# One normalisation in place of two in a row ahead of the token routes

## The reference, cut to what matters

```python
def _layernorm(x, axis=-1, eps=1e-05):
    m = jnp.mean(x, axis=axis, keepdims=True)
    v = jnp.var(x, axis=axis, keepdims=True)
    return (x - m) / jnp.sqrt(v + eps)

def _L1_ffn_ref(x, gamma, beta, Wr, br, W1, b1, W2, b2):
    mu = jnp.mean(x, axis=-1, keepdims=True)
    var = jnp.mean(jnp.square(x - mu), axis=-1, keepdims=True)
    xn = (x - mu) * jax.lax.rsqrt(var + EPS) * gamma + beta
    logits = jnp.einsum('bsd,de->bse', xn, Wr) + br
    top_vals, top_idx = jax.lax.top_k(logits, K)          # K = 2 of E = 8
    ...                                                   # the chosen experts on xn, weighted and summed

x = x + _L0_gnn_ref(_layernorm(x, axis=-1), ...)
x = x + _L0_ffn_ref(_layernorm(x, axis=-1)[None], ...)[0]
x = x + _L1_gnn_ref(_layernorm(x, axis=-1), ...)
x = x + _L1_ffn_ref(_layernorm(x, axis=-1)[None], ...)[0]
```

## Time and profile before

| | before |
|---|---|
| median of three executions | 6341.12 us |
| the profiled execution's own time | 6339.42 us |
| its span, first to last instruction | 6337.8 us |
| TensorE busy / VectorE busy | 4515.4 us / 3970.4 us |
| ScalarE busy / GpSimd busy | 2035.9 us / 2842.5 us |
| mean granted clock of TensorE (1 is 2.4 GHz) | 0.875 |

### The profile page before, as it was taken

How to read it: one execution, slowest core, us unless ns; L and a number is a source line. 1 busy time by engine, 2 the same in 40 slices (tenths; PEclk the granted TensorE clock), 3 DMA queues, 4 the chain that set the end, 5 groups by cost and what they waited for, 6 DMA issues and landing times. The chain is left out here.

```text
span 6337.8 us, 104789 instructions
## 1 busy us (share of the span) xinstructions
PE 4515.4 (71%) x23232; PEld 3431.3 (54%) x23437; DVE 3970.4 (63%) x7274; ACT 2035.9 (32%) x4728; POOL 2842.5 (45%) x2898
## 2 busy tenths in 40 slices
PE   0688888888778888888859779355555553439990
PEld 0556666666565666666649779343344342416660
DVE  4677777777667777777766656795444445713332
ACT  0134454545324555555533323320000000314440
POOL 0066666666107777777400010007777774061116
PEclk9999999999989999999979889687767776559995
DMA  6466556556236666666420030013333332122113
GB/s 88 141 185 181 173 171 176 173 174 174 81 129 200 187 182 183 180 184 183 127 91 0 0 103 0 10 36 103 104 103 103 104 104 68 42 96 71 61 55 121
DMA packets 352764, 736.54 MB, mean 116 GB/s; under 512 B 75533, under 2 KB 193809, under 8 KB 352477
## 3 DMA queue, kind: packets, MB, share of 16 engines
q0 software_dynamic: 189824, 588.23, 31.8%
q1 hardware_dynamic: 162782, 146.70, 8.1%
HBM read 634.25 MB, written 100.43 MB: 116 GB/s over the span
## 5 line engine op out<-in xcount | busy, mean ns | idle before, releaser
L967 POOL DMA_INDIRECT rows_a<-kv_scratch,att_idx x848 | 872.6, 1029 | 971.2 <-issue 540.9
L728 POOL DMA_INDIRECT rows_a<-k_scratch,sage_sum_idx x832 | 798.0, 959 | 856.2 <-issue 852.0
L967 POOL DMA_INDIRECT rows_c<-kv_scratch,att_idx x816 | 871.5, 1068 | 353.0 <-issue 245.0
L1425 PE MATMUL ps<-rows_a 128*128 128x258 f32 x1664 | 610.9, 532 | 469.9 <-DMA rows_a<-k_scratch,sage_sum_idx 310.9
L1105 PE MATMUL ps<-attention_rows_b,att_work 128*128 x3328 | 870.4, 403 | 77.5 <-DVE att_work L1213 37.4
L1024 ACT ACTIVATE attention_rows_b<-ps x1664 | 649.2, 390 | 598.0 <-PE ps L1119 374.0
L1425 PEld LDWEIGHTS ps<-rows_a 128*128 128x128 f32 x1664 | 419.4, 264 | 661.0 <-DVE sage_rows_b L1403 410.4
L1105 PEld LDWEIGHTS ps<-attention_rows_b,att_work 128*128 128x128 f32 x3328 | 612.3, 196 | 212.3 <-issue 125.2
L1403 DVE TENSOR_TENSOR sage_rows_b<-sage_rows_b,ps 128x258 f32 x832 | 353.0, 424 | 564.3 <-PE ps L1425 370.0
L1119 PE MATMUL ps<-rows_a,att_work 128*128 128x264 f32 x1696 | 516.6, 431 | 82.0 <-DVE rows_a L1227 63.8
L1119 PE MATMUL ps<-rows_c,att_work 128*128 128x264 f32 x1632 | 504.9, 431 | 55.3 <-issue 27.4
(11 more groups left out here) (396 smaller groups left out, 9295.8 us busy)
## 6 DMA issues: line engine op xcount, KB each, us to landing
kv_scratch<-rows_c SPq DMA_DIRECT2D x100, 256.0 KB
rows_a<-kv_scratch,att_idx POOLq DMA_INDIRECT x848, 3.7
slot_in<-rows_c SPq DMA_DIRECT2D x1, 13568.0 KB
rows_a<-slot_in SPq DMA_DIRECT2D x106, 128.0 KB
slot_out<-rows_a POOLq DMA_DIRECT2D x106, 128.0 KB
rows_a<-k_scratch,sage_sum_idx POOLq DMA_INDIRECT x832, 2.7
rows_c<-kv_scratch,att_idx POOLq DMA_INDIRECT x816
h_scratch<-rows_a SPq DMA_DIRECT2D x2, 6400.0 KB
```

Source lines behind the costliest of these rows:

```text
L728: pool.indirect_dma_start(ring[:, slot, 0:D], None, table, bass.IndirectOffsetOnAxis(ap=idx[:, slot:slot + 1], axis=0)).then_inc(landed[sl ...
L967: pool.indirect_dma_start(r.halves[h][:, u, 0:KV], None, c.kv_dram[:, :], bass.IndirectOffsetOnAxis(ap=idx[:, slot:slot + 1], axis=0)).the ...
L1425: mm = pe.matmul(c.ps[:, to:to + nw], s_buf[:, q, u, :], rhs, start=True, stop=True)
```

## The change

The call of `ln_x3` goes, and `ln_tok` reads `rows_c` in its place. With `normed_twice` two small operations more make v + eps*v + eps*eps out of v. In all eight calls eps is now added on VectorE by the second operand pair of an instruction that was there (L436), and the root on ScalarE has no bias column.

```diff
@@ -399,7 +399,8 @@
-def layer_norm(c, src, dst, name, have_stats=False, gamma=None, beta=None, add_to=None):
+def layer_norm(c, src, dst, name, have_stats=False, gamma=None, beta=None, add_to=None,
+               normed_twice=False):
@@ -433,7 +434,12 @@
                 do(v.scalar_tensor_tensor(c.rstd[:, :], tmp, D / 4.0, c.rstd[:, :], ALU.mult, ALU.add))
-                do(v.tensor_scalar(c.rstd[:, :], c.rstd[:, :], 1.0 / D, None, ALU.mult))
+                if normed_twice:
+                    do(v.tensor_scalar(c.rstd[:, :], c.rstd[:, :], 1.0 / D, None, ALU.mult))
+                    do(v.tensor_scalar(tmp, c.rstd[:, :], LN_EPS, LN_EPS * LN_EPS, ALU.mult, ALU.add))
+                    do(v.tensor_tensor(c.rstd[:, :], c.rstd[:, :], tmp, ALU.add))
+                else:
+                    do(v.tensor_scalar(c.rstd[:, :], c.rstd[:, :], 1.0 / D, LN_EPS, ALU.mult, ALU.add))
                 v.sem_inc(var_ready, 1)
@@ -461,7 +467,7 @@
-                a.activation(c.rstd[:, :], c.rstd[:, :], ACT.Sqrt, bias=c.eps_col[:, 0:1]).then_inc(rooted, 1)
+                a.activation(c.rstd[:, :], c.rstd[:, :], ACT.Sqrt).then_inc(rooted, 1)
@@ -2564,8 +2570,7 @@
-            layer_norm(c, c.rows_c, c.rows_a, "ln_x3")
-            layer_norm(c, c.rows_a, c.rows_a, "ln_tok", False, L1_ffn_gamma, L1_ffn_beta)
+            layer_norm(c, c.rows_c, c.rows_a, "ln_tok", False, L1_ffn_gamma, L1_ffn_beta, normed_twice=True)
```

## The result

The changed kernel took 6315.13 us (median of 6 runs, 6313.01 to 6319.74), the kernel before 6344.64 us (6 runs, 6338.59 to 6346.97). The ratio is 0.9956, with an interval from 0.9943 to 0.9969: 28 us less, between 20 and 36. The forecast was 30.4 us less and 6310 us, with a range of 6300 to 6320 us. The time lies inside, 5 us above the value. Of these 5 us, 3.5 belong to the kernel before: with three more executions its median rose from the 6341.12 us that the forecast started from to 6344.64 us. The saving by the ratio is 2.5 us smaller than the sum, which the interval of 16 us cannot tell from nothing; what follows goes by the lengths of stages.

What follows compares the result with a forecast made beforehand. VectorE was taken to bound both normalisations, with nothing beside to hide them. -30.88 + 0.48 = -30.4 us from the profiled 6339.4 gives 6309.0; the median, 1.7 us higher, gives 6310.7, predicted as 6310 us, range 6300 to 6320.

Steps and rivals of the forecast that it cites:

- No cover: In `ln_x3` and `ln_tok` VectorE bounds both calls, busy 28.43 of 30.9 us in `ln_x3`; nothing beside could hide them.
- 30.88 us from start to start: Removing `ln_x3` saves the distance from its statistics' start to those of `ln_tok`, 5394.30 - 5363.42 us, no part hidden.
- +0.48 us added: In `ln_tok`, two small chained operations on 128x50 cost 0.23 and 0.25 us, all on the path.
- The statistics from `rows_c`: In `ln_tok`, reading `rows_c` for `rows_a` may give 0.21 us; counted 0 to -0.2, taken as 0.
- The root: ScalarE's root without bias column, eight times: between 0 and 2.7 us less in all, taken as 0.
- The clock in `expert_rows`: TensorE's clock rise at the stage's start may come earlier or later against the work: -4.5 to +4.5 us.
- rival A: A faster TensorE clock in `token_routes`: 18 us more gain, about -48 us, 6291 us; chance 3%.
- rival D: `expert_rows` stays longer at 1.2 GHz, eating the gain from 61 us of low clock: 6345 us and above; chance 1%.
- Rival C: Half the removed time comes back through a late transfer or engine: about -15 us, 6325 us; chance 3%.
- "Otherwise the same" for the stages behind the change: `token_routes`, `dispatch`, `expert_rows` and `combine` start 30.4 us earlier and are otherwise the same, save for TensorE's clock.
- Rival B: Moved VectorE and ScalarE loops reload code, 2.7 us a pass in `token_routes` and `expert_rows`: 6357 us; 4% in two outcomes.
- All windows ahead of 5363 should be the same.: A sign to check: every timeline window before the removed normalisation, at 5363 us, keeps its length.

Runs made afterwards that it cites:

- The pads: Changed kernel plus semaphore increments: TensorE 4 (6310.98 us) or 24 (6317.09 us), GpSimd 8 (6312.66 us), SyncE 4 (6311.71 us).

## Why the prediction was right, and where it was not

- **No cover.** Right. 28.43 of 30.9 us of VectorE with TensorE and GpSimd at nothing meant what it said; once more cost 31.0 us, once less saved 30.8. The page's row of 40 slices does not show it, other than "Time and profile before" has it: a slice is 158 us, and in the two that hold this stretch TensorE reads 3 and 4 tenths and DMA 2 and 1; only GpSimd reads 0, in one of them.
- **30.88 us from start to start.** Right. GpSimd's wait at the barrier shrank by 30.9 us. Of the 1.18 us put down to the barrier a function by itself shows 0.8 us; no run takes the other 0.4 us apart.
- **+0.48 us added.** Right: 0.47 us. A second pair of immediates costs nothing, as was taken: 0.19 us with two (L439), 0.19 with one (L438).
- **The statistics from `rows_c`, taken at 0 between 0 and -0.2 us.** They took 16.43 us in place of 16.64, the whole 0.21 us. With this, 0.47 us added and 0.09 us off the root, `ln_tok` should take 0.2 us more than its 54.4 us; it took 54.5.
- **The root, taken at 0 between 0 and -2.7 us.** It was -0.6 us: the changed kernel has seven roots and not the eight that the working counts, since the eighth call is the one that went. The reason given (one element a partition more to read, so nothing) was wrong: the column cost 92 ns of 337.
- **The clock in `expert_rows`, -4.5 to +4.5 us.** Right in size, but the cause is chance. In the changed kernel the granted clock rose at 5688.9, 6 us behind the first matmul, against 10.5 us before, and the first interval was 4.29 us in place of 5.88. The kernel before did the same in its second profile (5.5 us, 4.45), so the change has no part in it. The granted clock of `token_routes` stayed at 0.50 to 0.52 in all profiles, so rival A did not come, and with `expert_rows` at 0.97 rival D neither. Rival C is out by the 30.8 us.
- **"Otherwise the same" for the stages behind the change.** This is the step that failed, by some 3 us. `dispatch` gained 1.1 us and `expert_rows` lost some 3 us in its loop and about 1 us behind it. The pads show that the 1.1 us and the loop's go by the position of code. Rival B had foreseen that moved code can cost something in every pass, but neither how nor how much: a pass pays 0.13 us and not the 2.7 us of a landing, and the delay is TensorE's, where B put it on VectorE and ScalarE. Its evidence, 119 and 39 packets of instructions, holds no more than that no pass loads code anew: the changed kernel has the same 119 and 39. The Trainium skill, Runtime: NRT & Kernel Launch (Instruction fetch mechanics), has a stall where the target of a taken branch must be fetched by DMA. No run here shows one: the delay of 0.13 us stands in the same place of each pass, with the packets unchanged.
- **"All windows ahead of 5363 should be the same."** Wrong: the first stretch varies by 7 us over thirteen profiles of the same instructions, and the neighbours' gather by 6. One pair of profiles can differ by that much; the medians are there to even it out.
- **The sum.** -30.8 for the normalisations, -0.6 for the six other roots, -1.1 for `dispatch` and about +4 for `expert_rows` make some -28.5 us, where the ratio says -28 and the two pairs of medians -29.5 and -24.6 us. That the time came within 5 us of the forecast is in part luck: the small terms, the clock's chance and the spread of the medians are a few us each. In the working, the terms below the forecast (2.9, 4.5 and 4) add up to 11.4 us, which makes the lower end 6299 and not 6301; and the rivals' times start from the profiled 6339.4 us, the forecast from the median, 1.7 us above it. Neither changes the forecast.

## What to carry to other kernels

Where only the step itself works between two barriers, as here, its price can be read off as one distance in the timeline, and doing the step once more measures the same price from the other side. What a change removes also moves the code behind it, on every engine that had a part in the removed barrier: compare the period of the loops behind, not only the stage that was edited. Here that was 1 us and 4 us of 6340. Before a few us of one profile are explained, the same kernel should be profiled twice.

## What the runs showed of the hardware

- The position of TensorE's instructions changed a loop's pass from 17.03 to 17.16 us, as a gap of 0.22 us put down to issue; four, eight or 24 instructions more ahead of the loop took it away. Eight on GpSimd changed `dispatch` from 156.2 to 157.3 us.
- A per-partition bias column costs ScalarE 92 ns on a root of 128x50 (337 against 245 ns).
- A function with eight semaphores and no work costs 0.8 us from barrier to barrier.
- Executions of the same instructions gave 184.8 to 192.2 us for the first stretch and 1060.4 to 1066.5 us for the neighbours' gather.
